# A three-layer interaction network: eight native weight tiles a pass, one product per group, slots released in two steps, and a reordered start

## What is computed

```python
for (W, b), split in zip(conv_params, split_flags):
    h = x.shape[1]
    z = jnp.einsum('bhd,bmd->bhmd', x, x0).reshape(B, h * x0.shape[1], D)
    xk = jax.nn.relu(jnp.einsum('oc,bcd->bod', W, z) + b[None, :, None])
    if split:
        half = xk.shape[1] // 2
        x, xk = (xk[:, :half], xk[:, half:])
    else:
        x = xk
    results.append(xk)
return jnp.sum(jnp.concatenate(results, axis=1), axis=2) @ Wo.T + bo
```

## Time and profile before

| | |
|---|---|
| median of 3 runs | 461.61 us (461.13 to 462.98) |
| the profiled execution | 461.44 us |
| its span | 459.4 us |
| granted PE clock, mean over the span | 0.992 |

### The profile page before, as it was taken

One profiled execution on the slowest core, in us unless ns is written; L12 is line 12 of the kernel. 1 busy time (PEld: TensorE's weight loads), 2 busy tenths in 40 slices (PEclk: granted clock), 3 DMA queues, 4 the chain that ended last, 5 costly groups with the idle time before them and its releaser, 6 DMA issues.

```text
span 459.4 us, 6013 instructions
## 1 busy us (share of the span) xinstructions
PE 447.3 (97%) x1602; PEld 299.0 (65%) x1602; DVE 418.3 (91%) x481; ACT 309.6 (67%) x389; POOL 394.2 (86%) x145
## 2 busy tenths in 40 slices
PE   7899599999999999999999999999999999999997
PEld 2344376667777676776767677676777767677774
DVE  3677589999999999999999999999999999999997
ACT  3752477868687685867758587775858768586661
POOL 0070388999989898998989899898989989999995
PEclk8999899999999999999999999999999999999999
DMA  7999987998959779595977959597694943822100
GB/s 277 236 225 220 228 176 171 216 218 190 223 126 222 156 166 223 114 228 120 221 161 164 224 112 228 116 226 163 158 229 102 239 103 78 190 46 48 33 12 0
DMA packets 22943, 75.66 MB, mean 165 GB/s; under 512 B 5779, under 2 KB 5907, under 8 KB 18836
## 3 DMA queue, kind: packets, MB, share of 16 engines
q1 hardware_dynamic: 22932, 75.52, 74.7%
HBM read 59.51 MB, written 0.00 MB: 130 GB/s over the span
## 4 chain that ended last, share of the span: by engine, by line
PE 92%; DMA 4%; ACT 1%; DVE 1%; issue 1%; SPq 1%; DVEq 0%; ACTq 0%
PE y_ps L854 28%; PE y_ps L842 16%; PE y_ps L844 16%; PE y_ps L860 16%; PE y_ps L850 7%; PE y_ps L818 4%; PE y_ps L866 4%; DMA a_rep<-x_sb 3%; DMA shifted<-x_dram 1%; DVE z L653 1%; PE y_ps L846 1%; PE y_ps L862 1%; SPq L364 0%; ACT results L475 0%; ACT x_sb L465 0%
## 5 line engine op out<-in xcount | busy, mean ns | idle before, releaser
L610 POOL TENSOR_TENSOR zl<-z,zh 128x1024 fp32r<-128x1024 f32 (+1 forms) x135 | 386.3, 2897 | 38.3 <-ACT zh L514 38.3
L653 DVE TENSOR_TENSOR z<-a_ps,b_fac 128x512 f32<-128x512 f32 (+2 forms) x256 | 273.4, 1092 | 21.5 <-PE y_ps L866 10.9
L514 ACT ACTIVATE zh<-z 128x1024 fp32r<-128x1024 f32 (+1 forms) x135 | 168.8, 1250 | 112.6 <-DVE z L653 112.1
L860 PE MATMUL y_ps<-zl,w_high 128*128 128x512 f32 x315 | 146.5, 557 | 0.0
L842 PE MATMUL y_ps<-zh,w_high 128*128 128x512 f32 x315 | 124.7, 396 | 4.7 <-ACT zh L514 4.7
L844 PE MATMUL y_ps<-zh,w_low 128*128 128x512 f32 x315 | 123.4, 392 | 0.0
L854 PE MATMUL y_ps<-z,w_raw 128*128 128x512 f32 x240 | 122.3, 591 | 0.0
L860 PEld LDWEIGHTS y_ps<-zl,w_high 128*128 128x128 f32 x315 | 59.0, 188 | 64.3 <-issue 56.3
L842 PEld LDWEIGHTS y_ps<-zh,w_high 128*128 128x128 f32 x315 | 59.2, 188 | 18.8 <-issue 5.7
L844 PEld LDWEIGHTS y_ps<-zh,w_low 128*128 128x128 f32 x315 | 59.4, 189 | 13.3 <-issue 0.2
L854 PEld LDWEIGHTS y_ps<-z,w_raw 128*128 128x128 f32 x240 | 45.1, 188 | 9.9
(11 more groups left out here) (55 smaller groups left out, 205.6 us busy)
## 6 DMA issues: line engine op xcount, KB each, us to landing
b_fac<-xt_dram SPq DMA_DIRECT2D x52, 512.0 KB, 8.7
shifted<-xt_dram SPq DMA_DIRECT2D x60, 256.0 KB, 4.9
a_rep<-x_sb SPq DMA_DIRECT2D x91, 128.0 KB, 2.6
shifted<-xt_dram SPq DMA_DIRECT2D x60, 128.0 KB, 5.1
b_fac<-xt_dram SPq DMA_DIRECT2D x16, 256.0 KB, 8.3
a_rep<-x_sb SPq DMA_DIRECT2D x62, 64.0 KB, 2.1
w_raw<-w_dram SPq DMA_DIRECT2D x2, 640.0 KB, 8.2
shifted<-x_dram SPq DMA_DIRECT2D x2, 512.0 KB, 5.5
```

Source lines behind the costliest of these rows:

```text
L514: nc.scalar.activation(zh[:, slot, 0:end - native, :], z[:, slot, native:end, :], ACT.Copy).then_inc(zh_ready, 1)
L610: nc.gpsimd.tensor_tensor(zl[:, slot, 0:end - native, :], z[:, slot, native:end, :], zh[:, slot, 0:end - native, :].bitcast(F32), ALU.subtract
L653: return nc.vector.tensor_tensor(dst, factor.unsqueeze(1).to_broadcast(list(dst.shape)), others, ALU.mult)
L860: mm = nc.tensor.matmul(y, wh[layer][:, w, :], zl[:, slot, t, :], start=False, stop=end_here)
```

## The change

Four parts.

- **Layer 3 of passes 3 to 15** splits all four tiles in its second and fourth group (`SPLIT[3]` = 3, 4, 3, 4) and gives one tile of every group to DVE (`BY_DVE[3]` = 1, 1, 1, 1). Eight tiles of a pass are then native. POOL's part of each group stays as large as it was (two or three tiles). The fourth part of zh and zl lies in new buffers (`FOURTH`). The last two passes keep the old split (`DRAIN_SPLIT`).
- **Layers 2 and 3** make all tiles of z of a group in one DVE instruction; `z_ready` follows the whole of it, and PE waits for it only through `zh_ready`.
- **A slot of z is released in two steps.** DVE's product of group q waits for POOL's subtract of group q-3 (`zl_ready`) and PE's last use of z and zh there (`front_used`); what writes zl (POOL, DVE's subtract) waits for PE's whole group (`group_used`).
- **The start** is reordered. All eight matmuls that pick chunk 0's fields stand at the front, three matmuls on zeros follow them, layer 1 of chunk 0 runs in two halves of its columns, each with its own bank, so that the first half of the factor of layer 2 can be made before the second half is done. ACT and SP take some copies and transfers of pass 2 earlier.

```diff
-SPLIT = {1: (2,), 2: (3, 3, 3, 3), 3: (3, 3, 3, 3)}
-BY_DVE = {1: (1,), 2: (1, 0, 1, 0), 3: (1, 0, 1, 0)}
-ZX_BANK = {0: 1, 1: 0, 3: 1, 5: 0, 7: 1}
+SPLIT = {1: (2,), 2: (3, 3, 3, 3), 3: (3, 4, 3, 4)}
+BY_DVE = {1: (1,), 2: (1, 0, 1, 0), 3: (1, 1, 1, 1)}
+DRAIN_SPLIT, DRAIN_BY_DVE = (3, 3, 3, 3), (1, 0, 1, 0)
+ZX_BANK = {0: 0, 1: 1, 3: 0, 5: 0, 6: 1, 7: 0, 8: 1}
+FOURTH = {6: 0, 8: 1}
...
@@ SP @@
+            spread(1, 1)
             load_b_half(2, 0)
-            spread(1, 1)
             load_b_half(2, 1)
             load_x(3)
...
@@ ACT, first group @@
+            def first_results():
+                act.wait_ge(y0_half_done, 1)
...
+                x, early = X_HALF[1], columns[0]
                 for to in (0, HALF):
+                    copy = nc.scalar.activation(a_ps[to:to + HALF, 0, early], y_ps[1][x, early], ACT.Relu,
+                                                bias=cols_sb[x, 0:1])
+                copy.then_inc(a0_half_in_psum, 1)
...
@@ ACT, pass 2 @@
+                        if pos == 5:
+                            x_to_sbuf(1, 1)
+                            results_to_sbuf(2, 0)
+                            results_to_sbuf(1, 1)
                         if pos == 6:
                             a_to_psum(3, 1, 0)
-                            results_to_sbuf(2, 0)
-                            y_to_sbuf(1, 1)
                         if pos == 7:
                             act.wait_ge(z_ready, groups_before(2) + 2)
+                            x_to_psum(2)
                             a_to_psum(2, 0, 1)
-                            x_to_psum(2)
...
                         if pos == 4:
+                            x_to_psum(3)
                             a_to_psum(2, 0, 2)
-                            x_to_psum(3)
...
@@ DVE, product @@
-                if not isinstance(q, int) or q >= RING:
+                if is_native(q - RING):
                     dve.wait_ge(group_used, q - (RING - 1))
+                elif not isinstance(q, int) or q >= RING:
+                    dve.wait_ge(zl_ready, splits_before(q - RING + 1))
+                    dve.wait_ge(front_used, splits_before(q - RING + 1))
...
-                multiply(z[:, slot, native:end, :], factor, others[:, pool:pool + end - native, :]).then_inc(z_ready, 1)
+                if layer > 1:
+                    multiply(z[:, slot, 0:end, :], factor, others[:, 0:end, :]).then_inc(z_ready, 1)
...
-                multiply(z[:, slot, 0:native, :], factor, others[:, 0:native, :]).then_inc(z_native_ready, 1)
+                if layer == 1:
+                    multiply(z[:, slot, 0:native, :], factor, others[:, 0:native, :]).then_inc(z_front_ready, 1)
...
@@ DVE, subtract; POOL has the same new wait @@
+                if not isinstance(q, int) or q >= RING:
+                    dve.wait_ge(group_used, q - (RING - 1))
                 dve.wait_ge(zxh_ready, e + 1)
...
@@ PE @@
             pick_b(0)
+            pick_b(1)
+            for _ in range(WARM):
+                nc.tensor.matmul(y_ps[1][:, 0:2 * P], pooled3[:, 0:P], pooled3[:, 0:2 * P], start=True, stop=True)
...
-                    pe.wait_ge(z_native_ready, q + 1)
+                    if layer == 1:
+                        pe.wait_ge(z_front_ready, c + natives_before(q))
                     for t in range(native):
...
+                    mm.then_inc(front_used, 1)
```

More of the change, by code:

```diff
@@ L509, in body @@
                         (pos, layer, g, q, e), k = here[pos]
-                        slot, (native, end, by_dve) = slot_of(i, k), parts_of(layer, g)
+                        slot, (native, end, by_dve) = slot_of(i, k), parts_of(i, layer, g)
                         act.wait_ge(z_ready, q + 1)
@@ L607, in body @@
                         continue
-                    slot, (native, end, by_dve) = slot_of(i, k), parts_of(layer, g)
+                    slot, (native, end, by_dve) = slot_of(i, k), parts_of(i, layer, g)
+                    if not isinstance(q, int) or q >= RING:
+                        pool.wait_ge(group_used, q - (RING - 1))
                     pool.wait_ge(zh_ready, splits_before(q) + 1)
@@ L654, in multiply, with first_product, product @@
                                                ALU.mult)
-            def product(i, step, k):
+            def first_product(slot, others, factor):
+                for n, bank0, done in ((columns[0], None, (z1_half_ready, z1_half_ready)),
+                                       (columns[1], y0_banks[1], (z_front_ready, z_ready))):
+                    if bank0 is None:
+                        dve.wait_ge(a0_half_in_psum, 1)
+                    else:
+                        dve.wait_ge(group_used, 1)
+                        x = X_HALF[1]
+                        for to in (0, HALF):
+                            copy = nc.vector.tensor_scalar(a_ps[to:to + HALF, 0, n], bank0[x, n], cols_sb[x, 0:1], 0.0,
+                                                           ALU.add, ALU.max)
+                        copy.then_inc(a_in_psum[2][0], 1)
+                    for t, signal in zip((0, NATIVE_CUT), done):
+                        if bank0 is not None and t == 0:
+                            dve.wait_ge(a_in_psum[2][0], 1)
+                        multiply(z[:, slot, t:t + NATIVE_CUT, n], factor[:, n], others[:, t:t + NATIVE_CUT, n]
+                                 ).then_inc(signal, 1)
+            def product(i, step, k, held):
                 pos, layer, g, q, e = step
-                c, slot, (native, end, by_dve) = i - (layer - 1), slot_of(i, k), parts_of(layer, g)
+                c, slot, (native, end, by_dve) = i - (layer - 1), slot_of(i, k), parts_of(i, layer, g)
                 if layer == 1:
@@ L720, in subtract @@
+                if not isinstance(q, int) or q >= RING:
+                    dve.wait_ge(group_used, q - (RING - 1))
                 dve.wait_ge(zxh_ready, e + 1)
-                nc.vector.tensor_tensor(zl[:, slot, end - native, :], zx_ps[:, ZX_BANK[pos], :],
-                                        zh[:, slot, end - native, :].bitcast(F32), ALU.subtract
+                nc.vector.tensor_tensor(dve_part("low", pos, slot, end - native), zx_ps[:, ZX_BANK[pos], :],
+                                        dve_part("high", pos, slot, end - native).bitcast(F32), ALU.subtract
@@ L728, in body @@
                 for pos in positions(i):
                     if pos in here:
[L730 to L734 removed]
+                        product(i, *here[pos], 1 if waiting else 0)
+                    if waiting:
+                        subtract(*waiting)
+                    waiting = (i, *here[pos]) if pos in here and has_subtract(i, here[pos][0]) else None
@@ L865, in body @@
                         pe.wait_ge(zxl_ready, e + 1)
-                        mm = nc.tensor.matmul(y, wh[layer][:, x_weights, :], zl[:, slot, x_part, :],
+                        mm = nc.tensor.matmul(y, wh[layer][:, x_weights, :], dve_part("low", pos, slot, x_part),
                                               start=False, stop=last)
```

181 lines of the change are left out of this document (120 added, 61 removed).

## The result

The changed kernel takes **460.0 us** (median of 20 runs, 458.41 to 461.24), the kernel before 461.7 beside it: 0.995 of its time, 95% interval 0.9936 to 0.9963. It is 1.7 us faster where 7.3 were forecast, and outside the range.

What follows compares the result with a forecast made beforehand. PE was taken to bound the passes, and DMA transfers the start. Eight native tiles -4.5, the start -3.5 and refilling +0.7 sum to -7.3 against 461.44: 454.1 us, own range 452 to 456.5, 8 in 10 range 449.3 to 458.

Steps and rivals of the forecast that it cites:

- -3.5: From the start to a mark in pass 3: the group that ended at 79.63 ends 3.5 us earlier.
- The term that was mis-sized: Start of pass 3: chunk 3's load lands near 61.5 us, bounds 60.5 and 62, as the DMA engines had no gap.
- A step on the way: Start of pass 2: PE begins its layer 1 near 46.5 instead of 53.30, 7 us gained at this point.
- the clock term of 0: Pass 3's layer 1: PE waits about 2 us, slower matmuls run beside POOL's path; 0 to 1 us, taken as 0.
- DVE fits, with 0.35 to spare: Each changed pass: DVE has about 26.25 us of work against PE's 26.6, so PE stays the bound.
- the ring has room: Slots of z: product, rounding and POOL's work after a release add to 6.8 us, against 8.8 for three groups of PE.
- the tile was sized 0.17: Passes 3 to 15: each of 26 swapped tiles saves PE 0.17 us, 4.5 us in all, if PE stays the bound.
- The end keeps its split: 0.: Last passes: the old split is kept there, so the end changes by 0 us.
- +0.7 for refilling: Passes 3 to 5: POOL has no lead over PE there, which costs 0.7 us, bounds 0 and 2.
- DVE takes over: Rival, chance 0.08: in each pass DVE's work plus kept waits makes 27.3 us, slower than before; 464.5 us in all.
- The start gains nothing: Rival, chance 0.14: ACT's rounding for pass 3 stands behind a copy awaiting a late spread, so pass 3 starts as before; 457.4 us.
- The transfers are no bound: Rival, chance 0.13: a deeper queue is served faster, so pass 3 starts when PE gets there; 449.6 us.

## Why the prediction was wrong

**Right in the mechanism of the start, lucky in its size.** The load of chunk 3 bounds it, the path runs over `x_ps` to DVE, `a_ps` of pass 2 is copied at 44.67 (forecast near 45), the product of four tiles ends 8.0 us after pass 3's start, as said, and moving the load in the queue moves pass 3. The profiled run gives -3.04 against -3.5. But its load came in early, and at the same mark the six kernels that share the program up to there stand between 76.59 and 78.65, 77.7 on average: a gain of 1.9 (the kernel before has one profile, 79.63). The term that was mis-sized is the load: near 61.5 with bounds of 60.5 and 62, but in four of the six `x_ps` begins only between 62.69 and 63.98, on average of all at 63.0. Why it lands so differently stays open. The median of 460.0 lies 1.0 above the profiled 459.04, much as this would have it.

A step on the way was wrong and stayed hidden. PE was to begin pass 2 near 46.5, 7 us earlier than before; it began at 49.71, 3.6 earlier. The second half of layer 3 of chunk 0 came late, and after that pause of 2.37 us PE's granted clock was 0.58 up to 43 us and 0.50, the lower level of 1.2 GHz, from there to 45. Timeline of PE, then a window:

```profile
41.47 8.80 PE L941 MATMUL y_ps<-z,w_raw 128*128 128x512 f32 x16 [2.37 <-DVE z L700]
```

```profile
43.00:45.00 2.00, 2.00 (x4) 0.90 (x3) 2.00 (x3) 0.33 (x1) 0.00 (x0) 0.50 1.18 266
```

ACT still waited 1.91 us for chunk 3 at 61.92, so this cost nothing. The pause that was forecast ahead of pass 3's layer 1 did not come in its place, and the clock term of 0 held.

**Wrong: "DVE fits, with 0.35 to spare" and "the ring has room".** This is the failed step behind the largest loss: 1.8 us came of 3.8 in passes 4 to 14. DVE's work was sized about rightly: 26.25 forecast without the ends that stick out, 26.42 busy with them where the passes don't alternate. The step that failed is the test of the fit: each engine's sum, and the way of one slot from release to use, against PE's pass. Both fit. What doesn't is the chain through DVE's run, ACT, POOL and PE that closes only after two passes, 53.54 on average against PE's 53.28. Merging two products into one lengthened it: ACT waits for four tiles where three would do. It cost 0.13 a pass, 1.4 us in eleven. Beside that the tile was sized 0.17 and is 0.145, so PE's pass is 26.64, not 26.6; that is the other 0.6.

**Wrong: "The end keeps its split: 0."** The split of layer 3 in passes 16 and 17 is kept, but not what stands ahead of it: the last group of pass 15 now has a subtract, and pass 16 no product to cover it. It cost 1.0 of the 1.4 us by which this stretch missed; with the subtract and the reduce moved it takes 64.6, where 64.5 were forecast.

**Near in size, wrong in part of the cause: +0.7 for refilling.** In the profiled run it was 1.7, within the bounds of 0 and 2. Some of that was a spread behind a load, which I had looked for only in pass 2: 1.1 in this run. In the three other runs with the same program the stretch from pass 3's mark to pass 4 took 19.07 to 19.33 instead of 20.05, which makes the term 0.7 to 1.0. What is left without the spread's stall is 0.6; that it is POOL's missing lead is not shown.

The range's own terms, load, refill and clock, add up to 452.4 to 456.9 and not to 452 to 456.5; 460.0 lies outside either.

**The rivals.** None came. "DVE takes over" named the kind of mechanism, waits that stay and move to POOL and ACT, and its 27.3 a pass is close to the 27.46 of the run with the one-step release; what kept the changed kernel from it is the release in two steps. "The start gains nothing" feared ACT's copy behind the spread: in the changed kernel it follows at 62.47 without a wait. It does wait, 3.18 us, once the load is moved ahead. "The transfers are no bound" fell with the load that landed at 61.9 and with the run that moved it.

The Trainium skill, page "DMA: Bandwidth & Descriptors", section "Specifications", gives about 358 GB/s as one core's limit to HBM; if that were the rate, the load would have landed an estimated 20 us earlier. The trace stays far below it with the DMA engines busy throughout: window of the run with chunk 3's load moved ahead, 243 GB/s at a busy share of 1.01:

```profile
4.00:56.00 52.00, 49.80 (x156) 26.99 (x155) 39.82 (x45) 27.17 (x45) 16.06 (x8) 1.00 1.01 243
```

## What to carry to other kernels

When a change brings the sums of two or three engines within a few per cent of each other, test it by loops, not by sums: follow one release through all engines until it meets itself, over two passes if need be, and ask of each merged instruction who waits for a part of it. Go through the first and last passes one by one, and look for the instruction whose cover is missing there. And in a queue that is full, each transfer has a place: move one ahead, and name the one that is then late. Before a difference of 1 us at the start is called an effect, look at the same stretch in other runs of the same program.

## What was not expected

PE counts as busy in all of a pass that holds 0.27 us of waits for POOL; only a slower triple of matmuls in the chain (0.79 and 0.83 instead of 0.69) and the weight loads' waits show them. The same program up to a load starts what waits for it up to 2.1 us apart, 61.92 to 63.98. And the zeros ahead of layer 1 do nothing: without them PE is busy from 6 to 10 us all the same, and the granted clock is 1.00.
